# Two attention stages whose projections stand in other cycles of the batch

## The reference, cut to what matters

```
q = norm(x) @ Wq.T + bq;  k = ctx @ Wk.T + bk;  v = ctx @ Wv.T + bv
layer 2: q, k turned by the rotary tables (x * cos + rotate_half(x) * sin)
scores = q k^T / 4          (layer 3: + mask * -1e15)
out = softmax(scores) v @ Wo.T + bo
x = x + tanh(gate) * out
```

## Time and profile before

| | |
|---|---|
| median of three runs | 3043.08 us |
| the profiled execution | 3048.9 us |
| its span | 3047.1 us |
| PE busy | 2778.5 us, 91% |
| DVE busy | 1549.9 us, 51% |
| ACT busy | 1301.9 us, 43% |
| POOL busy | 608.1 us, 20% |

### The profile page before, as it was taken

The page is one execution under the profiler, slowest core; times in us unless marked ns, Lnnn a source line. Parts: engine busy times, 40 slices in busy tenths (PEclk is TensorE's granted clock), DMA queues, the critical chain, the costliest instruction groups (busy, mean ns, idle before and its releaser), DMA issues. The chain is left out here.

```text
span 3047.1 us, 58569 instructions
## 1 busy us (share of the span) xinstructions
PE 2778.5 (91%) x20336; PEld 2123.1 (70%) x20336; DVE 1549.9 (51%) x4191; ACT 1301.9 (43%) x3619; POOL 608.1 (20%) x553
## 2 busy tenths in 40 slices
PE   6999968999999999798999975999988999769998
PEld 4777645666666666655666655999986777658887
DVE  4767643555555555344777753233326777532222
ACT  4777621444334334212666641333326777312221
POOL 1566530000000000000434320222210000013222
PEclk9999979999999999689999975999999999769999
DMA  3000010000000000010000004999971000048886
GB/s 113 17 21 17 6 67 2 12 12 7 12 12 8 11 12 1 28 31 2 22 17 22 17 17 142 335 326 327 328 246 29 22 22 17 25 158 284 284 278 222
DMA packets 92312, 269.13 MB, mean 88 GB/s; under 512 B 25657, under 2 KB 51402, under 8 KB 77738
## 3 DMA queue, kind: packets, MB, share of 16 engines
q1 hardware_dynamic: 74858, 244.10, 23.3%
q0 software_dynamic: 13632, 18.62, 3.1%
q10 hardware_dynamic: 3616, 3.67, 0.4%
HBM read 249.70 MB, written 18.48 MB: 88 GB/s over the span
## 5 line engine op out<-in xcount | busy, mean ns | idle before, releaser
L2189 PE MATMUL e_ab_ps<-e_xT,e_w 128*128 128x128 f32 (+1 forms) x3968 | 469.8, 279 | 5.8 <-DMA e_w<-in_L2f_w 2.1
L2189 PEld LDWEIGHTS e_ab_ps<-e_xT,e_w 128*128 128x128 f32 (+1 forms) x3968 | 455.8, 190 | 25.0 <-issue 12.1
L748 PEld LDWEIGHTS a_full_ps<-ident,a_probs 112*125 112x125 f32 x2688 | 372.4, 190 | 123.6 <-issue 64.3
L748 PE MATMUL a_full_ps<-ident,a_probs 112*125 112x112 f32 x2688 | 420.0, 281 | 19.4 <-ACT a_pT L861 8.4
L855 ACT ACTIVATE a_probs<-a_masked,a_negmax 112x375 f32<-112x375 f32 x512 | 305.4, 598 | 278.0 <-DVE a_negmax L1071 278.0
L1097 DVE COPY a_pT<-a_full_ps 125x448 f32<-125x448 f32 x448 | 278.2, 622 | 284.1 <-PE a_full_ps L748 281.1
L649 PE MATMUL a_full_ps<-attention_room 128*125 128x256 f32 (+1 forms) x960 | 331.2, 474 | 9.7 <-ACT a_qT L847 3.7
L641 PE MATMUL a_full_ps<-attention_room 128*128 128x375 f32 x896 | 324.8, 491 | 0.7 <-DVE a_v L1027 0.6
L1071 DVE CUSTOM_DVE_ANT_0 a_masked<-a_sc_ps,a_mask_add 112x375 f32<-112x375 f32 x512 | 249.9, 545 | 42.0 <-PE a_sc_ps L735 41.6
L855 ACT ACTIVATE a_probs<-a_sc_ps,a_negmax 112x375 f32<-112x375 f32 x384 | 217.9, 579 | 120.7 <-DVE a_negmax L1077 120.7
L735 PE MATMUL a_sc_ps<-a_kT,a_qT 32*112 32x375 f32 (+1 forms) x1792 | 241.2, 512 | 20.9 <-ACT a_probs L855 13.7
(11 more groups left out here) (253 smaller groups left out, 3697.1 us busy)
## 6 DMA issues: line engine op xcount, KB each, us to landing
e_w<-in_L2f_w SPq DMA_DIRECT2D x105, 1024.0 KB, 6.4
e_w<-in_L3f_w SPq DMA_DIRECT2D x72, 704.0 KB
e_w<-in_L3f_w SPq DMA_DIRECT2D x36, 768.0 KB, 5.8
attention_room<-in_ctxT SPq DMA_DIRECT2D x64, 375.0 KB, 3.1
e_b<-in_L2f_b SPq DMA_DIRECT2D x35, 128.0 KB, 7.9
p_rows<-r_kept SPq DMA_DIRECT2D x32, 112.0 KB, 1.8
p_sums<-x_all ACTq DMA_DIRECT2D x2, 1792.0 KB, 17.8
attention_room<-in_L0x_spline_wT SPq DMA_DIRECT2D x1, 2048.0 KB, 10.3
```

The lines of the kernel that those rows point to most:

```text
L748: mm = pe.transpose(full_ps[0:KT, bank_of["turn", i, k], (j % 4) * S:(j % 4 + 1) * S], probs[:, i % 2, a, t * KT:(t + 1) * KT], ident[0:S, ...
L2189: mm = pe.matmul(ab_ps[0:rows[f], (par * FC + f) % RING, i * SLOTS:(i + 1) * SLOTS], w[:, par, c, f * P:f * P + rows[f]], xT[:, c, :], sta ...
```

## The change

The table `CYCLES` gets other rows for layers 2 and 3; no other line changes.

```diff
@@ CYCLES
-    2: [[[], [("k", 0)], [("v", 0, 0)], [("xT",)]],
+    2: [[[], [("k", 0)], [], [("xT",)]],
         [[], [("q", 0)], [("out",)], []],
-        [[], [("v", 1, 0)], [], []],
-        [[], [("k", 1)], [("v", 2, 0)], [("rt",)]]],
-    3: [[[], [("k", 0)], [("v", 0, 0)], [("xT",)]],
+        [[], [("k", 1)], [("v", 0, 0)], []],
+        [[], [("v", 1, 0)], [("v", 2, 0)], [("rt",)]]],
+    3: [[[], [("k", 0)], [], [("xT",)]],
         [[], [("out",)], [("q", 0)], []],
-        [[], [("v", 1, 0)], [], []],
-        [[], [("k", 1)], [("v", 2, 0)], [("rt",)]]],
+        [[], [("k", 1)], [("v", 0, 0)], []],
+        [[], [("v", 1, 0)], [("v", 2, 0)], [("rt",)]]],
```

## The result

The changed kernel takes 3060.01 us, the median of six runs (3055.46 to 3062.20). The kernel before, run beside it, takes 3047.83 us (3041.56 to 3050.14). The ratio is 1.0049, with a 95% interval of 1.0038 to 1.0059: slower by 0.49%, where the forecast was +0.49%. Since the kernel before read 4.8 us higher here than in its first three runs, the absolute time came out 2 us over the forecast of 3058. The profiled execution has a span of 3057.8 us, 10.7 more than before.

The account below looks back on a forecast made before the run. PE was the busiest engine in both layers, with cycle 0 ended by xn and layer 2's cycles 2 and 3 by ScalarE. Layer 3 +11.9, layer 2 +2.9, other terms 0: 3043.1 + 14.8 = 3058 us (+0.49%), range 3049 to 3066.

Parts of the forecast that it names:

- Cycle 0 stays (the main step): Cycle 0, both layers: xn from VectorE sets its end, so removing v0 gains 0; stays 5.73 (layer 3) and 5.92 us.
- Cycle 2: Now k1 and v0: layer 3 4.11 to 5.20 us by PE's work, layer 2 5.09 to 5.47 by ScalarE's chain.
- Cycle 3: Now v1 and v2, v2 waiting for ScalarE's copy: layer 3 5.40 to 5.10 us, layer 2 5.47 to 5.28.
- The periods and the sum: Batches of 20.97 us (layer 3, +0.79) and 21.99 (layer 2, +0.19), 15 times: +11.9 and +2.9, total +14.8 us.
- The start-ups: Batch before the first, each layer: same matmuls, taken as 0, at most one v (0.87 us) either way.
- The rule of the Trainium skill on small idles: Cycling PSUM banks with frequent small idles can swing PE between half and full clock; could cost more than the waits.
- The ends: a term that I had put at nothing: Last batch of each layer: only batches 0 to 14 carry projections and were counted, with no term for the last.
- The clock in the steady part: Rival: longer cycle 0 wait drops layer 2's clock to 0.68 for 5 us a batch, +24 us, 3082 us; 5%.
- the earlier xn: Rival: xn comes as soon as PE is ready, cycle 0 shortens in both layers, -9 us, 3034 us; 6%.
- half of it: Rival: xn comes some 0.4 us earlier in both layers, total +3 us, 3046 us; 6%.

Follow-up runs that it names:

- e3: Changed kernel with v0 back in cycle 0 of both layers (cycle 2 has k1 alone, cycle 3 v1 and v2): ratio 1.0012 to the kernel before.
- e10: Kernel before, with VectorE taking the next batch's norm statistics in cycle 3 and writing xn right after cycle 0's division: ratio 0.9955 to before.
- e12: Changed kernel, with VectorE taking the next batch's norm statistics in cycle 3 and writing xn right after cycle 0's division: ratio 0.9963 to before.
- e4: Changed kernel, but in layer 2 VectorE instead of ScalarE copies k1 out of PSUM: ratio 1.0032 to the kernel before.
- e2: Kernel before with the new table row in layer 3 only: ratio 1.0038 to the kernel before.
- e7: Kernel before, with norm statistics taken early in cycle 2, xn after cycle 0's division, and VectorE copying k0 and k1 in layer 2: ratio 0.9970 to before.
- e9: Changed kernel, with norm statistics taken early in cycle 2, xn after cycle 0's division, and VectorE copying k0 and k1 in layer 2: ratio 0.9919 to before.
- e13: Kernel before, with norm statistics taken early in cycle 3, xn after cycle 0's division, and VectorE copying k0 and k1 in layer 2: ratio 0.9936 to before.

## Why the prediction was right

**Cycle 0 stays (the main step): right, shown.** Forecast 5.73 and 5.92 with waits of 1.0 to 1.2 us and about 1.24; measured 5.73 and 5.94, 1.04 and 1.24. e3 shows that v0 is free in cycle 0, e10 and e12 that it is xn that makes it free.

**Cycle 2: right.** Forecast 5.20 and 5.47, measured 5.22 and 5.48. That it is ACT's chain in layer 2 is shown by e4, where the cycle fell to 5.16.

**Cycle 3: right.** Forecast 5.10 and 5.28, measured 5.10 and 5.28. In layer 2 v2 starts 3.60 after the scores and not 3.70 as I had worked out (1557.37 to 1560.97), and the cycle is 5.28 all the same; the steps behind v2 came out 0.1 us longer (1.68 from v2 to the scores, where I had 1.58). In layer 3 v2 starts at 3.43, not 3.52, with the same offset. Two errors of 0.1 us that cancel: for a matmul that starts behind a wait, the trace's start is not the point from which the durations of an unbroken stream may be added. The short wait in front of v2 that the prediction named shows in layer 2, where v2's weight load stands 0.26 us for ScalarE's pT copy; in layer 3 the trace has none.

**The periods and the sum.** 20.99 us a batch where 20.97 was forecast, and 22.03 where it was 21.99. Layer 3's attention grew by 12.7 us in all, forecast 11.9; layer 2's by 0.4, forecast 2.9, for a reason that the forecast did not hold (the ends, below). The ratios agree: +0.38% for layer 3 alone, +0.07% for layer 2 alone.

**The start-ups: the term that was too small.** I took 0 and at most one v (0.87 us) either way in each layer. Measured +1.1 and +3.2 us, since I had counted the moved work and not the clock. The k1 pair, at 1.2 GHz, took 2.87 us instead of 1.53. In layer 3 e3 tests what does it, as it has the new table but v0 in front of the first xT. Its first scores come 9.8 us after the stage's first matmul (L790), against 9.6 before the change and 12.9, 11.4 and 13.0 in the three profiles without v0 there (changed, e2, e4). Its k1 pair takes 1.53 us again. So in layer 3 it is the missing v0 that costs the time. The 0.2 us left in e3 go with k1, which stands there in the place of the shorter v1, in front of the first scores. In layer 2 v0 does not decide it: e3 has 12.8 us, the kernel before 12.1, the kernels without v0 there 12.6 to 13.2.

The rule of the Trainium skill on small idles (TensorE: Matmul & The Clock Gate, section "A second HAM failure mode: psum-queue depth-cycling"), which I had weighed for the steady part, did not show there: one wait of 1.24 us in a batch of 22 us left the clock at 1.00.

**The ends: a term that I had put at nothing.** The sum has 15 batches and nothing for the last one, which has no next batch and does the same work in both kernels. But the table reaches it all the same. A bank belongs to a place in the table, whether its use is run or not, and so the table still says what a turn waits for. From the last scores to the end of the last output projection layer 2 takes 14.11 us before (1786.42 to 1800.53), at a granted clock of 0.67:

```profile
1790.15 0.66 PE L748 MATMUL a_full_ps<-ident,a_probs 112*125 112x112 f32 x4 [1.01 <-ACT a_pT L861]
1791.62 1.35 PE L766 MATMUL a_o_ps<-a_pT,a_v 125*32 125x112 f32 x24 [0.81 <-DVE a_pT L1097]
```

and 9.70 after (1792.92 to 1802.62), at 1.00:

```profile
1794.51 1.56 PE L748 MATMUL a_full_ps<-ident,a_probs 112*125 112x112 f32 x12
1796.97 0.78 PE L766 MATMUL a_o_ps<-a_pT,a_v 125*32 125x112 f32 x24 [0.90 <-DVE a_pT L1097]
```

In cycle 2 of the old table turn 2 stands three places behind turn 0, and waits 1.01 us for its copy; in the new one k1 stands there, which the last batch does not have, and the three turns run in one piece. e3 has the old places in this cycle, and its profile has them at full clock: the same wait of 1.01, and 10.84 us at 1.00. So of the 4.4 us that the last stretch of layer 2 became shorter 1.1 are the bank and 3.3 the clock. In layer 3 the same stretch takes 13.03 us before and 9.89 after; e7 has the old places there at full clock, 10.63 us, so 0.7 are the banks and 2.4 the clock. The new places also cost something: turn 2 of cycle 0 now stands three places behind turn 0, and cycles 0 and 1 of the last batch are 0.45 us longer in layer 3 (8.02 to 8.47), level in layer 2. The 3.7 and 1.6 us of the section on the profile are smaller than these gains, since they also hold the longer cycles 2 and 3 of the batch before and stop at the last weight load.

Why the clock falls stays open. Over the fourteen kernels the last stretch (from the last L735 of the stage to its end) ran below 1.00 in ten of the fourteen attention stages with the old places and in none of the fourteen with the new ones; in e9 it fell one cycle earlier, behind the wait of turn 2 in cycle 0 (1.06 us), and was back at 1.00. So the fall comes with the waits of the old places, but they do not decide it alone: e3 and e13 have them in layer 2, and e7 in both layers, at 1.00. The starts (+4.3) and the ends (-5.3) cancel to within 1 us, and so the total fits better than its parts deserve: that is luck.

**The rivals.** The clock in the steady part (3082), the earlier xn (3034) and half of it (3046) did not come. The second of them is what e12 builds by an edit, and the gain that the prediction gave it for layer 3, 0.79 - 1.16 = -0.37 us a batch, is what e12 measures: 19.78 against 20.18, -0.40; in layer 2 -0.26 both.

## What to carry to other kernels

Work that stands in front of a wait costs nothing there, however uneven the stages look; before dealing it out evenly, find what ends each stage, and move only from stages that the engine itself ends to stages that wait. Even then ask whether the moved work makes that wait longer: cycle 2 of layer 2 had 0.89 us of waiting, and grew by 0.39 with k1 in it, because k1's copy stands among the exponentials that PE waits for. If such a wait is to be used, first make the awaited thing earlier: the same table cost 12 us with a late xn, 2 us with an early one, and gained 5 to 8 us once ScalarE's chain was shortened too. Where buffers go round by places in a list, look also at the first and the last batch, which leave some places empty. When a step is added to another engine's queue in a short cycle, look at what stands behind it there: the same statistics cost 0.6 us a batch in a cycle of 4.11 us and nothing in one of 5.40.

## What the runs showed of the hardware

A PE wait of 1.24 us in every batch of 22 us left the granted clock at 1.00 over 320 us. At the start of a stage, where the clock is at 0.50, one projection less (0.87 us at full clock) held it there for some microseconds more: 0.50 and 0.85 in two windows where it had been 0.65 and 1.00. At the end of a stage the same order of work with the same waits of 1.01 and 0.81 us ran once at 1.00 (e3, 10.84 us) and once at 0.67 (before, 14.11 us).

The copy of a k (128 x 375) takes ScalarE 0.57 us in the trace, and in the middle of its chain of exponentials it lengthened the cycle by 0.39 us over one with a v copy (5.48 against 5.09). From the end of ScalarE's exponential to the start of the scores that wait for it there are 0.14 us, from the end of xn on VectorE to the transpose 0.14 to 0.15.
